# A Toeplitz convolution with nine blocks per head in place of ten, inside a fused attention and mixture-of-experts kernel

## The reference

```python
kv = einsum('bhil,bhjl->bijhl', ctx_, ctx_)            # per head: all products of its 8 rows
y = irfft(rfft(kv, 2L) * rfft(taps, 2L))[..., :L]      # causal convolution along l, L = 512
out = einsum('bijhl,bhil->bjhl', y + kv * D, layernorm(x))
x = x + out
x = x + moe_and_shared_ffn(layernorm(x))               # 16 experts, top 4, capacity 256, plus a shared FFN
```

## Time and profile before

| | |
|---|---|
| median of three runs | 641.5 us |
| profiled execution: time | 642.93 us |
| its span in the profile | 641.1 us |
| granted TensorE clock, mean | 0.983 of full |
| PE busy | 594.9 us, 93% |
| PE weight loads busy | 562.4 us, 88% |
| DVE busy | 479.0 us, 75% |
| POOL busy | 350.5 us, 55% |
| ACT busy | 283.1 us, 44% |
| chain that ended last: share of PE, DVE, POOL | 78%, 7%, 5% |

### The profile page before, as it was taken

How to read it: one execution, slowest core, us unless ns; L and a number is a source line. 1 busy time by engine, 2 the same in 40 slices (tenths; PEclk the granted TensorE clock), 3 DMA queues, 4 the chain that set the end, 5 groups by cost and what they waited for, 6 DMA issues and landing times.

```text
span 641.1 us, 13621 instructions
## 1 busy us (share of the span) xinstructions
PE 594.9 (93%) x4487; PEld 562.4 (88%) x4487; DVE 479.0 (75%) x1234; ACT 283.1 (44%) x503; POOL 350.5 (55%) x477
## 2 busy tenths in 40 slices
PE   2857999999999999999999989899999999999993
PEld 2846898999999999999999878889999999999992
DVE  5898879758758678677679858898887877888640
ACT  3343542423423423424333242556556655665641
POOL 5797698666857667676662263225334444333342
PEclk9988899999999999999999999999999999999997
DMA  5655513414325115222130061958888877888643
GB/s 157 213 141 180 170 61 98 133 35 120 111 67 145 51 65 164 65 81 82 33 100 34 5 197 35 318 175 243 244 243 237 227 215 217 236 233 234 167 53 47
DMA packets 50386, 90.31 MB, mean 141 GB/s; under 512 B 3920, under 2 KB 20304, under 8 KB 50336
## 3 DMA queue, kind: packets, MB, share of 16 engines
q1 hardware_dynamic: 43168, 72.89, 36.6%
q0 software_dynamic: 7168, 16.78, 12.5%
HBM read 72.71 MB, written 16.94 MB: 140 GB/s over the span
## 4 chain that ended last, share of the span: by engine, by line
PE 78%; DVE 7%; POOL 5%; issue 4%; DMA 3%; ACT 2%; SPq 0%; POOLq 0%; DVEq 0%; ACTq 0%
PE gu L535 16%; PE yb L472 15%; PE gu L672 12%; PE mb L687 10%; PE gu L565 7%; PE yb L672 7%; PE mb L452 4%; PE yb L452 2%; POOL kvl L1036 2%; POOL kv L1028 2%; DMA xg<-normalised_tokens,slot_rows 1%; DMA toep<-toeplitz_taps 1%; PE yb L646 1%; ACT kvh L788 1%; DVE oT L1249 1%
## 5 line engine op out<-in xcount | busy, mean ns | idle before, releaser
L472 PE MATMUL yb<-kvh,toep 128*128 128x288 f32 x640 | 138.9, 304 | 8.5 <-DVE prod L1235 3.4
L535 PE MATMUL gu<-xT,sw 128*128 128x256 f32 (+2 forms) x1152 | 142.3, 282 | 0.0
L535 PEld LDWEIGHTS gu<-xT,sw 128*128 128x128 f32 (+2 forms) x1152 | 138.2, 181 | 0.3
L472 PEld LDWEIGHTS yb<-kvh,toep 128*128 128x128 f32 x640 | 108.4, 195 | 9.9 <-issue 8.5
L1028 POOL TENSOR_TENSOR kv<-kT 128x256 f32 (+3 forms) x248 | 114.6, 500 | 0.0
L1036 POOL TENSOR_TENSOR kvl<-kv,kvh 128x1152 fp32r<-128x1152 f32 x31 | 83.1, 2679 | 55.2 <-ACT kvh L788 55.1
L1233 DVE TENSOR_TENSOR prod<-yb,qT 128x96 f32<-128x96 f32 (+11 forms) x288 | 78.7, 284 | 42.4 <-PE yb L472 41.3
L472 PE MATMUL yb<-kvl,toep 128*128 128x288 f32 x320 | 96.7, 302 | 0.0
L788 ACT ACTIVATE kvh<-kv 128x1152 fp32r<-128x1152 f32 x32 | 37.4, 1168 | 93.9 <-POOL kv L1028 50.1
L1249 DVE TENSOR_REDUCE oT<-prod 128x256 f32<-128x2048 f32 x32 | 72.9, 2278 | 0.1
L1235 DVE TENSOR_TENSOR prod<-yb,qT 128x96 f32<-128x96 f32 (+10 forms) x252 | 67.6, 268 | 0.0
(11 more groups left out here) (175 smaller groups left out, 1019.8 us busy)
## 6 DMA issues: line engine op xcount, KB each, us to landing
toep<-toeplitz_taps SPq DMA_DIRECT2D x32, 512.0 KB, 3.7
raw_w<-in_L_ffn_w_gate_dram SPq DMA_DIRECT2D x16, 704.0 KB, 8.3
raw_w<-in_L_ffn_w_up_dram SPq DMA_DIRECT2D x16, 704.0 KB, 9.6
raw_d<-in_L_ffn_w_down_dram SPq DMA_DIRECT2D x16, 512.0 KB, 4.3
c_t<-in_ctx_dram SPq DMA_DIRECT2D x16, 256.0 KB, 4.7
x_t<-in_x_dram SPq DMA_DIRECT2D x16, 256.0 KB, 5.2
normalised_tokens<-xn SPq DMA_DIRECT2D x16, 256.0 KB, 2.9
out_dram<-yo SPq DMA_DIRECT2D x16, 256.0 KB, 3.0
```

What stands on the lines that cost most here:

```text
L472: last = pe.matmul(yb[:, lb, 0:PW], toep[s][:, a, d:d + P], rhs[:, s, m, :], start=(i == 0), stop=(i == len(steps) - 1))
L535: last = pe.matmul(gu[0:m, i % 2, u * GT:(u + 1) * GT], sw[:, c, a, col:col + m], xT[:, c, b, :], start=(c == 0 and (a, b) == PASSES[0]), ...
```

## The change

From head 8 on (`PLAIN = 2 * GH`, the third group) the convolution has another form. Write T0..T3 for the Toeplitz blocks and k0..k3 for the pair blocks. The third and fourth output blocks share T2 (k0 + k1):

- block 2 = T2 (k0 + k1) + (T1 - T2) k1 + T0 k2
- block 3 = T2 (k0 + k1) + (T3 - T2) k0 + T1 k2 + T0 k3

That is 1 + 2 + 2 + 3 block products and one for T2 (k0 + k1). The differences of taps are built once by DVE at the start (`steps_of`, `stephl`), stored to memory by SP and loaded per head as `tstep` beside a narrower `tlast`. POOL adds the two pair blocks as a fifth block of `kv`, which ACT and POOL then round and split along with the others. The shared product has 288 columns and the free room of a bank of `yb` is 224, so PE writes it in two pieces, 224 columns behind output block 0 and 64 behind block 1. ACT copies both to `zs` (`copy_z`), and DVE adds `zs` to output blocks 2 and 3 in place (`join`) before `multiply`. `prod` has one buffer in place of two, and some tables of the start lie elsewhere.

```diff
+    KB = LB + 1
+    ZA = 512 - PW
+    PLAIN = 2 * GH
@@ sync
+                if plain(n):
+                    src = bass.AP(h.tensor, h.offset, [[1, P], [TW, 2], [1, L]])
+                    sp.dma_start(toep[k][:].bitcast(fp32), src).then_inc(toep_in[k], 16)
+                else:
+                    src = bass.AP(h.tensor, h.offset + P, [[1, P], [TW, 2], [1, L - P]])
+                    sp.dma_start(tlast[k][:].bitcast(fp32), src).then_inc(toep_in[k], 16)
...
+                    sp.dma_start(tstep[k][:].rearrange("p h d c -> p (h d) c").bitcast(fp32), src)\
+                        .then_inc(toep_in[k], 16)
...
             load_group(1)
+            sp.wait_ge(steps_hl, 1)
+            sp.dma_start(step_dram, stephl[:].rearrange("n h d c -> n (h d) c").bitcast(fp32)).then_inc(steps_out, 16)
             load_shared(0)
             load_shared(1)
@@ tensor, convolve
+                        block = lambda k: lambda a: tlast[s][:, a, (LB - 2 - k) * P:(LB - 1 - k) * P]
+                        step = lambda k: lambda a: tstep[s][:, a, k, :]
+                        terms = (((0, block(0)),), ((0, block(1)), (1, block(0))), ((1, step(1)), (2, block(0))),
+                                 ((0, step(0)), (2, block(1)), (3, block(0))))[lb]
...
+                    if not plain(n) and lb == 1:
+                        for z, (lo, hi) in enumerate(((0, ZA), (ZA, PW))):
+                            for a, b in PASSES:
+                                end = pe.matmul(yb[:, z, PW:PW + hi - lo], block(2)(a), (kvh, kvl)[b][:, s, LB, lo:hi],
+                                          start=((a, b) == PASSES[0]), stop=((a, b) == PASSES[-1]))
+                        end.then_inc(z_mm, 1)
@@ scalar
+                nb = LB if plain(n) else KB
+                act.activation(kvh[:, s, 0:nb, :], kv[:, s, 0:nb, :], ACT.Copy).then_inc(kv_h, 1)
+            def copy_z(n):
+                if not plain(n):
+                    act.wait_ge(z_mm, n - (PLAIN - 1))
+                    for z, (lo, hi) in enumerate(((0, ZA), (ZA, PW))):
+                        last = act.activation(zs[:, lo:hi], yb[:, z, PW:PW + hi - lo], ACT.Copy)
+                    last.then_inc(z_cp, 1)
@@ gpsimd, pairs and low_kv
+                    last.then_inc(kv_p, 1)
+                    pool.wait_ge(kv_p, n - (PLAIN - 1))
+                    pool.tensor_tensor(kv[:, s, LB, :], kv[:, s, 0, :], kv[:, s, 1, :], ALU.add).then_inc(kv_m, 1)
...
+                pool.tensor_tensor(kvl[:, s, 0:nb, :], kv[:, s, 0:nb, :], kvh[:, s, 0:nb, :].bitcast(fp32), ALU.subtract)\
@@ vector
+            def join(n):
+                if not plain(n):
+                    dve.wait_ge(conv, n + 1)
+                    dve.wait_ge(z_cp, n - (PLAIN - 1))
+                    both = yb[:, 2:LB, 0:PW]
+                    dve.tensor_tensor(both, both, zs[:].unsqueeze(1).broadcast_to([P, 2, PW]), ALU.add).then_inc(z_ok, 1)
...
             def steps(g, prep, post, chunk, extra=()):
+                join(GH * g)
                 if chunk:
                     add_x(g - 1)
...
                 for hl in range(1, GH):
+                    join(GH * g + hl)
                     multiply(GH * g + hl, g, hl)
@@ vector, start, ahead of steps(0, ...)
+            dve.tensor_tensor(steps_of[:, 0, :], pad[:, 0:2 * P], pad[:, P:3 * P], ALU.subtract)
+            link(dve.tensor_tensor(steps_of[:, 1, :], pad[:, 2 * P:4 * P], pad[:, P:3 * P], ALU.subtract))
+            link(dve.tensor_copy(stephl[:, 0, :, :], steps_of[:]))
+            dve.tensor_tensor(stephl[:, 1, :, :], steps_of[:], stephl[:, 0, :, :].bitcast(fp32), ALU.subtract)\
+                .then_inc(steps_hl, 1)
+            dve.wait_ge(steps_hl, 1)
```

More of the change, by code:

```diff
@@ L154, in xattn_moe_kernel @@
         qT = place("qT", [P, 2, LB, GR * B], fp32)
[L155 to L158, removed]
+        kv = place("kv", [P, 2, KB, PW], fp32)
+        kvh = place("kvh", [P, 2, KB, PW], fp32r)
+        kvl = place("kvl", [P, 2, KB, PW], fp32r)
+        toep, tlast, tstep = [], [], []
+        for n in range(2):
+            toep_at = cursor[0]
+            toep.append(place(f"toep{n}", [P, 2, L], fp32r))
+            cursor[0] = toep_at
+            tlast.append(place(f"tlast{n}", [P, 2, L - P], fp32r))
+            tstep.append(place(f"tstep{n}", [P, 2, 2, P], fp32r))
+        zs = place("zs", [P, PW], fp32)
         oT = place("oT", [P, LB, GR * B], fp32)
         prod_at = cursor[0]
-        prod = place("prod", [P, 2, LB, HD * B // 2, HD, 2], fp32)
+        prod = place("prod", [P, LB, HD * B // 2, HD, 2], fp32)
+        prod_end = cursor[0]
         cursor[0] = prod_at
@@ L165, in xattn_moe_kernel @@
         pad = place("pad", [H, TW], fp32)
+        skip_t = place("skip_t", [H, 1], fp32)
+        steps_of = place("steps_of", [H, 2, 2 * P], fp32)
+        assert cursor[0] <= prod_end
+        cursor[0] = xT_at
         padhl = place("padhl", [H, 2, TW], fp32r)
-        skip_t = place("skip_t", [H, 1], fp32)
         gate_rows = place("gate_rows", [E, L], fp32)
+        col_i = place("col_i", [P, P], int32)
+        colmod_i = place("colmod_i", [P, P], int32)
+        assert cursor[0] <= sil_at
+        cursor[0] = sil_at
+        stephl = place("stephl", [H, 2, 2, 2 * P], fp32r)
+        assert cursor[0] <= stage_at
         PADW = E + 8
@@ L283, in low_done, with plain @@
                 eng.wait_ge(sw_l, DVE_PIECES.index(piece) + 1)
+        def plain(n):
+            return isinstance(n, int) and n < PLAIN
         def by_halves(n):
@@ L827, in steps @@
                 early = isinstance(g, int) and g == 1
+                copy_z(GH * g)
                 if not early:
@@ L842, in steps @@
                     split_shared(piece)
+                copy_z(GH * g + 1)
                 if not early:
@@ L852, in steps @@
                     round_kv(GH * g + 3, 1)
+                copy_z(GH * g + 2)
                 if prep and not early:
@@ L1035, in low_kv @@
                 pool.wait_ge(kv_m, n)
-                pool.tensor_tensor(kvl[:, s, :, :], kv[:, s, :, :], kvh[:, s, :, :].bitcast(fp32), ALU.subtract)\
+                nb = LB if plain(n) else KB
+                pool.tensor_tensor(kvl[:, s, 0:nb, :], kv[:, s, 0:nb, :], kvh[:, s, 0:nb, :].bitcast(fp32), ALU.subtract)\
                     .then_inc(kv_l, 1)
@@ L1232, in blocks @@
                         second = q[:, lo:hi, d * B:HD * B].rearrange("p c (a u) -> p c a u", u=2)
-                        last = dve.tensor_tensor(prod[:, s, lo:hi, d * B // 2:HD * B // 2, d, :], pair, first, ALU.mult)
+                        last = dve.tensor_tensor(prod[:, lo:hi, d * B // 2:HD * B // 2, d, :], pair, first, ALU.mult)
                         if d:
-                            last = dve.tensor_tensor(prod[:, s, lo:hi, 0:w // 2, HD - d, :], pair, second, ALU.mult)
+                            last = dve.tensor_tensor(prod[:, lo:hi, 0:w // 2, HD - d, :], pair, second, ALU.mult)
                     return last
@@ L1445, in _ @@
             dve.wait_ge(kv_h, 1)
-            dve.tensor_tensor(kvl[:, 0, :, :], kv[:, 0, :, :], kvh[:, 0, :, :].bitcast(fp32), ALU.subtract)\
+            dve.tensor_tensor(kvl[:, 0, 0:LB, :], kv[:, 0, 0:LB, :], kvh[:, 0, 0:LB, :].bitcast(fp32), ALU.subtract)\
                 .then_inc(kv0_l, 1)
```

49 lines of the change are left out of this document (32 added, 17 removed).

## The result

The changed kernel takes 648.69 us (median of six runs, 646.62 to 649.9), the kernel before 641.57 us beside it: ratio 1.0104, 95% interval 1.0086 to 1.0122, or 7.1 us slower. The forecast was 645.2 us, slower. The profiled execution took 648.29 us with a span of 646.0. Against the profiled execution of the kernel before (642.93, span 641.1) that is 5.4 us: 4.9 in the spans and 0.5 around them (2.3 us in place of 1.8).

What follows compares the result with a forecast made beforehand. PE was taken to bound loop groups 3 to 6, other engines the start, passage and last head. 1.8 + 2.7 + 1.7 - 2.5 = +3.7 us gave 646.6, less 1.4 to the median: 645.2 us; range 643 to 648, 8 in 10 639 to 651.

Steps and rivals of the forecast that it cites:

- Short matmuls stream slowly: Rival on PE's convolution: short matmuls run at the transposes' 0.85 ns per column; +8.5 us, 650.0 us, chance 0.12.
- the forecast's mechanism: In PE's convolution a short matmul costs 113 ns whatever its columns, from its weight load; forecast's chance 0.50.
- PE per head: Each changed head's convolution on PE takes 3.86 us, saving 0.12; 21 heads count, 2.5 us saved.
- the cheap one: Rival on PE's convolution: short matmuls cost in proportion to their columns; -2.2 us, 639.3 us, chance 0.15.
- the two on places: Rivals: start's delay absorbed, +1.9, 643.4 us, chance 0.13; passage and last group cost half, +1.5, 643.0 us, chance 0.10.
- the start: DVE's tap differences hold up SP's store and the shared weights, so head 2's rounding comes late; +1.8 us.
- the passage: Into group 2: added POOL and ACT work for heads 8 and 9 makes PE's `down` wait; +2.7 us.
- the last group: DVE's joins there make PE wait before head 31 and delay the last sum; +1.7 us.
- the load's 107 ns: On PE, a load of 128 weight columns takes its columns over 1.2, by the Trainium skill.
- the gap formula: On PE, a lone matmul stream takes N / 2.4 + 2.5: 96 and 29 ns, saving about 0.4 us per head.
- a landing: At the start, time from SP's issue of the shared weights to their arrival, taken as 4.4 us.

Runs made afterwards that it cites:

- gap: Changed kernel with DVE's first three tap-difference instructions moved into its wait for ACT's first rounding; 646.23 us, ratio 1.0067 to the kernel before.
- loads_first: Changed kernel with SP issuing the shared weights' loads ahead of its wait for the tap differences and their store; 646.35 us, ratio 1.0071 to the kernel before.
- after: The changed kernel itself, with all of the change, against the kernel before; 648.69 us, ratio 1.0104.
- tail_plain: Changed kernel with the last four heads, 28 to 31, in the old ten-block form; 648.09 us, ratio 1.0099 to the kernel before.
- z_three_pieces: Changed kernel with the shared product in three pieces of 96 columns in place of 224 and 64; 657.5 us, ratio 1.0255 to the kernel before.
- from_12: Changed kernel with the nine-block form beginning at head 12, one group later; 645.51 us, ratio 1.0059 to the kernel before.

## Why the prediction was nearly right

The time lies in the range of 8 in 10 (639 to 651), though outside the 643 to 648 that the prediction gave its own forecast, and it is nearer to the 650.0 of the rival *Short matmuls stream slowly* than to 645.2. It is the loop group of 43.93 us, and not the time, that speaks for the forecast's mechanism.

**PE per head: right.** Forecast 3.86 us, saving 0.12, group 43.9; measured 3.87, 0.12 and 43.93. The short matmuls are 98 ns apart and not 113, but the other 24 take 3.28 us and not 3.18: the two errors cancel, the second being in where one piece ends and the next begins. Both rivals on the columns fell, the cheap one (-2.2 us) and the dear one (+8.5 us). So did the two on places: the start was not absorbed, and the passage and the last group cost 2.9 and 1.7 us and not half of 4.4. On the rules of the Trainium skill that the prediction cites from "TensorE: Matmul & The Clock Gate": the load's 107 ns is near the 98 and 104 ns measured, and the gap formula's 29 ns at 64 columns did not hold here; the section "Back-to-back issue gap" itself says that for pairs of load and matmul the formula is too low at few columns, which the prediction left out.

**The start: the mechanism right, one term wrong.** The term is "about 0.33, 0.33, 0.45 and 0.65 us with small gaps, so they end near 18.85": the last one measured 3.02 us, and they ended at 21.48. With 21.9 in place of 19.2 for the first issue and a landing of 4.2 us, which was well estimated, head 2 is 4.0 us late and PE 3.5. The first `down` came 4.5 us late just as forecast, which is luck: a half clock that missed `gate_up` gave back what the start cost over its forecast. The estimate took a DVE duration from a place where POOL was idle (L1436 in the earlier trace rows; POOL ran nothing between 4.1 and 10.1 us) and used it beside a POOL subtraction. The trace of before held the warning, in DVE and POOL at 77 us:

```profile
77.46 2.62 DVE L1204 TENSOR_SCALAR xnm<-xmv 128x2 f32<-128x2 f32 x1
```

```profile
77.39 2.66 POOL L1036 TENSOR_TENSOR kvl<-kv,kvh 128x1152 fp32r<-128x1152 f32 x1 [3.70 <-ACT kvh L788]
```

Two columns in 2.62 us; the same instruction takes 0.17 at the start. Those traces and gap's agree with a rule that the prediction should have weighed: the Trainium skill, "SBUF — State Buffer", section "SBUF: two separate sides", says that the port pair which VectorE and GpSimd share is "an **exclusive lock**, not a bandwidth split", held for the whole instruction by whichever starts first; on VectorE's side it names instructions with two SBUF inputs, as the subtraction has, and its two-port modes.

**The passage: right.** 2.7 us forecast, 2.9 in the trace of loads_first, 3.3 in the four whose `gate_up` had no half clock. The excess is in the adds: with its own semaphore an add puts the next rounding 0.94 us later (85.69 to 86.63 in loads_first), not 0.8.

**The last group: right.** 1.7 forecast, 1.74 by the sum given under loads_first.

**What no step had: some 1.6 us.** The terms as measured are 3.5 + 2.9 - 2.5 + 1.74 = 5.6 us, and the medians differ by 7.1. 0.47 us lie around the span: 2.2 to 2.3 us in the kernels with 24 changed heads, 2.0 to 2.2 with 20, 1.8 with 16 or none. Its cause is open. The rest goes by the clock, as far as the traces show: half clock lay over `down` in three of the five kernels that had the long wait in front of it (after, tail_plain, gap), at 1.6 to 2.7 us each, by their stretch to the last sum over the 257.45 us of loads_first (tail_plain over 255.95, its 19 heads' saving off before's), and in none of the five traces without it. The mean granted clock says the same over all runs: 0.9793 in the six of the changed kernel, 0.9821 in the fourteen of the kernel before that ran in the first session. By that the changed kernel has some 3.6 us more at half clock, which cost 1.8 us at most, an estimate. That the wait brings the half clock on is not shown; loads_first and z_three_pieces had the wait without it.

So the forecast of 645.2 was 3.5 us low, of which 1.7 are the DVE instruction, 0.5 the time around the span, 0.2 the passage, and the rest, 1.1, is put down to the clock, which is argued and not shown.

## What to carry to other kernels

Count matmuls with their weight loads as well as columns: nine blocks in 30 matmuls are worth 3% of the convolution, not 10%. Before adding a VectorE instruction on SBUF data, see in the trace what GpSimd runs at that moment, since the instruction may last as long as GpSimd's does, and see what stands behind it in a queue of loads. A saving of 0.12 us per head in a bound loop is soon spent at the ends, where other engines set the time: here the form gained only when it was kept to the 16 heads in the middle and the start's delay was taken away.

## What the runs showed of the hardware that was not expected

- A VectorE subtraction of 512 columns in 32 rows took 0.68 us ahead of GpSimd's subtraction and 3.02 us when it began 0.42 us behind its start. Even 256 columns took 0.78 beside GpSimd's products, 0.41 alone.
- Rounded 32-bit matmuls of 64 and 224 columns, each with a load of 128 weight columns, follow each other every 98 ns on average at the full clock, and those of 96 columns every 104 ns.
- The half clock moves between kernels that differ only in small delays, and it is worth up to 2.7 us by the work that it falls on: `gate_up`'s 48 matmuls took 5.87 us without it, and 6.47 to 7.62 with it. Even the traces of after and from_12, whose kernels do the same work up to there, had 5.87 and 7.62.
